# A transformer layer on eight cores: the attention product is copied off its PSUM bank before it is scaled, the prologue works in token halves, and projections, weight buffers and transposes are re-ordered

## The chip, the cores and the metric

The kernel runs on the 8 NeuronCores of one Trainium2 chip, two dies of four cores. Every core computes one of the 8 batch entries with the same program and no core talks to another. The metric is the time of the slowest core in microseconds (us), as measured on the device; several executions are timed and the median is quoted. Engines are named as the profile names them: PE is TensorE (its weight loads are PEld), DVE is VectorE, ACT is ScalarE, POOL is GpSimd, SP is SyncE. SP and POOL only issue DMAs here; an issue on such a queue is written SPq or POOLq. Each engine runs its instructions strictly in program order and waits on semaphores.

## The reference

Per core: x is 2048 tokens by 2048 features in float32. Attention has 16 heads of 128. Half of each head's features is rotated (RoPE) in the queries and keys. The feed-forward block has 5632 hidden features and integer weights that are read as (w - 128) * scale.

```python
q, k, v = (proj(wq), proj(wk), proj(wv))
q, k = apply_rope(q, k, sin, cos)
att = jnp.einsum('bhqd,bhkd->bhqk', q, k) * (1.0 / math.sqrt(HD))
att = jax.nn.softmax(att, axis=-1)
y = jnp.einsum('bhqk,bhkd->bhqd', att, v)
y = y.transpose(0, 2, 1, 3).reshape(b, t, c)
return y @ wo.T
...
gate = jax.nn.silu(_qlinear(x, wq_gate, s_gate))
up = _qlinear(x, wq_up, s_up)
return _qlinear(gate * up, wq_down, s_down)
...
x = _layernorm(x + _L0_attn_ref(...))
x = _layernorm(x + _L0_ffn_ref(...))
```

## The kernel before

The program is written by hand, engine by engine; the order in the source is the order on the engine. One array AB in SBUF holds all tiles at hand-chosen byte offsets, and PS is the PSUM, used as eight banks of 128x512 float32. So the profile calls nearly every operand AB or PS, and the line tells what it is. All matmuls are 128x128 by 128x512 in bfloat16; there are 14656 of them. The stages, in order of time:

**Prologue.** POOL loads the weights wv and wk of head 0, then the transposed input xT in 16 tiles of 128 features by 2048 tokens (L388), casting to bfloat16. PE accumulates V and K of head 0 in all eight banks as the tiles arrive (L448, 128 matmuls), then makes the queries of head 0 (64 matmuls of L455).

**Attention.** There are 64 blocks m of 512 queries (4 per head), each of 8 slots of 256 keys, so 512 slots s. In a slot PE computes the scores of the next slot (2 matmuls, L480, banks 0 to 3), then 6 matmuls of a projection job (L455, banks 6 and 7), then the product of the probabilities with V (2 matmuls, L522), which accumulates over the 8 slots of a block in bank 4 or 5 by the parity of m. A job is 16 matmuls and makes 512 tokens of Q, K or V of the next head; the last head has none. ACT takes the exponential of the scores (L620) into a ring of 8 buffers P and copies each finished job to SBUF (L645). DVE adds the exponentials up (L734, L738, L743), rotates Q and K (L696 to L706), and scales the product (L727).

The softmax denominator of block m goes a long way: PE sums over the keys with a matmul by ones (`key_sums`, L491) in slot 9 after the block's start, into the job bank that is idle then; ACT copies one row of it (`sums_row`, L627); SP spreads that row over partitions (L281); DVE takes the reciprocal (`recip`, L720, slot 12); SP stores it to HBM (L285) and loads it back broadcast to 128 partitions (L292, the tile RB); DVE multiplies bank 4 or 5 by RB (`y_scale`, L727, slot 15) and so frees the bank. The next-but-one block starts on that bank in slot 16, and its first product matmul waits for the multiplication:

```python
if k == 0:
    if m >= 2:
        t.wait_ge(dve_y, m - 1)
```

SP stores y to HBM and at the end loads it back for all heads as YTB (L304). V jobs are written transposed, and SP turns them with DMA transposes (L256).

**Output projection.** 16 token tiles of 64 matmuls (L544) with the weights WO; the last eight of those are loaded in one burst when the jobs are done (L407). DVE adds x and takes the layer-norm sums, ACT normalises, SP and POOL store the result in float32 (x1f) and bfloat16 (x1b), and SP loads it back transposed (X1T, L331).

**Feed-forward, twice for 1024 tokens each.** Gate and up projections, 44 x 64 matmuls (L565, L571), then the down projection in 4 passes of 352 matmuls (L578). The down weights arrive in 44 tiles in a ring of 4 buffers (POOL, L438), and DVE subtracts 128 from each (L768). At the start of the first half's down projection SP issues 16 DMA transposes in a row, which bring X1T for the second half (L351); behind them on SP stand the stores and loads of the residual (L356, L346) for which DVE's additions wait (L830). In the last pass DVE finishes each tile of 128 tokens alone: scale, add, statistics, wait for ACT's square root, then normalise one half while ACT normalises the other (`finish_tile`, L679, L867).

## Time and profile before

| | |
|---|---|
| time, median of 3 runs | 3418.36 us (3415.16, 3418.36, 3443.7) |
| the profiled execution | 3445.24 us, with a span of 3443.7 us on its slowest core |
| spans of the 8 cores in it | 3367.0 to 3443.7 us |
| matmuls | 14656, busy 3216.7 us, 93% of the span |
| DVE, ACT, POOL busy | 38%, 23%, 6% of the span |
| wait of PE ended by DVE's L727 | 111.4 us before L522 and 5.2 us before L544 |
| wait of PE ended by DVE's L768 | 37.4 us |

The profile describes one execution on its slowest core, core 1. Matmuls are pipelined: each shows some 380 ns of busy time, and in an unbroken stream one starts about every 216 ns. The busy share of PE over the whole span is a mean over stages that differ, so the stages are looked at one by one below.

### The profile page before, as it was taken

How to read it: one execution, taken by the hardware profiler on the slowest of the kernel's cores; microseconds unless marked ns; L12 is line 12 of the kernel's file. 1: busy time of each engine (PE TensorE's matmuls, PEld its weight loads, DVE VectorE, ACT ScalarE, POOL GpSimd, SP SyncE). 2: the span in 40 equal slices, each digit the busy share in tenths (PEclk: the TensorE clock that was granted, in tenths of full speed). 3: DMA queues.
4: the chain of work that ended last, by engine and by line, in shares of the span. 5: the costliest groups of instructions: out<-in, count | busy, mean ns of one | idle time of the engine just before them, and what ended most of it. 6: DMA issues, size and time to landing. Idle time of an engine off the chain costs nothing.

```text
span 3443.7 us, 40018 instructions; the slowest of 8 cores (3367.0 to 3443.7 us)
## 1 busy us (share of the span) xinstructions
PE 3216.7 (93%) x14656; PEld 1436.6 (42%) x14656; DVE 1311.1 (38%) x1504; ACT 804.6 (23%) x904; POOL 205.2 (6%) x364
## 2 busy tenths in 40 slices
PE   6998999999999957999999999969999999999997
PEld 2443443444444422444444444434444444444443
DVE  1665665666666643342111121022232221121334
ACT  0554554555555541111000000000010000000001
POOL 1000000000000000000100100000000001000000
PEclk9999999999999988999999999989999999999998
DMA  9333333333233154996555655996556655433555
GB/s 159 47 52 50 64 53 50 55 52 54 51 51 47 27 98 129 253 240 126 78 80 76 98 76 80 93 127 127 110 135 147 147 103 106 74 62 57 103 111 158
DMA packets 189534, 327.50 MB, mean 95 GB/s; under 512 B 97952, under 2 KB 114336, under 8 KB 183072
## 3 DMA queue, kind: packets, MB, share of 16 engines
q0 software_dynamic: 51840, 188.77, 34.4%
q1 hardware_dynamic: 137504, 136.17, 18.3%
q8 instruction: 123, 2.02, 0.3%
q14 instruction: 67, 0.55, 0.1%
HBM read 429.47 MB, written 58.85 MB: 142 GB/s over the span
## 4 chain that ended last, share of the span: by engine, by line
PE 75%; DMA 13%; SPq 4%; DVE 3%; issue 3%; ACT 1%; POOL 0%; DVEq 0%; ACTq 0%; another core or an unknown queue 0%; POOLq 0%
PE PS L565 18%; PE PS L571 18%; PE PS L578 14%; PE PS L455 11%; DMA AB<-rl_sp 8%; PE PS L544 6%; PE PS L522 4%; PE PS L480 4%; SPq L351 4%; DMA rl_sp<-AB 3%; DMA AB<-xT 1%; DMA AB<-AB 1%; ACT AB L620 1%; DVE AB L727 1%; DVE AB L738 1%
## 5 line engine op out<-in xcount | busy, mean ns | idle before, releaser
L455 PE MATMUL PS<-AB 128*128 128x512 bf16 x2944 | 722.8, 383 | 1.5 <-DVE AB L685 1.5
L620 ACT ACTIVATE AB<-PS 128x1024 bf16<-128x1024 f32 x512 | 524.2, 1025 | 574.3 <-PE PS L480 556.5
L578 PE MATMUL PS<-AB 128*128 128x512 bf16 x2816 | 615.8, 382 | 40.2 <-DVE AB L768 37.4
L565 PE MATMUL PS<-AB 128*128 128x512 bf16 x2816 | 623.8, 380 | 2.5 <-DVE AB L764 2.5
L571 PE MATMUL PS<-AB 128*128 128x512 bf16 x2816 | 622.1, 379 | 0.0
L738 DVE TENSOR_TENSOR AB<-AB 128x1024 f32<-128x1024 f32 x384 | 469.8, 1223 | 302.8 <-ACT AB L620 298.4
L795 DVE SCALAR_TENSOR_TENSOR AB<-PS,AB 128x1024 bf16<-128x1024 f32 x88 | 113.0, 1284 | 963.4 <-PE PS L571 963.4
L455 PEld LDWEIGHTS PS<-AB 128*128 128x128 bf16 x2944 | 290.0, 99 | 355.7 <-issue 13.3
L578 PEld LDWEIGHTS PS<-AB 128*128 128x128 bf16 x2816 | 276.6, 98 | 379.1 <-issue 52.3
L669 ACT ACTIVATE AB<-PS,AB 128x1024 f32<-128x1024 f32 x88 | 98.2, 1116 | 1433.8 <-PE PS L565 1433.8
L522 PE MATMUL PS<-AB 128*128 128x512 bf16 x1024 | 312.8, 388 | 120.6 <-DVE AB L727 111.4
L565 PEld LDWEIGHTS PS<-AB 128*128 128x128 bf16 x2816 | 275.9, 98 | 336.1 <-issue 5.2
L571 PEld LDWEIGHTS PS<-AB 128*128 128x128 bf16 x2816 | 275.5, 98 | 332.4
L480 PE MATMUL PS<-AB 128*128 128x512 bf16 x1024 | 310.9, 386 | 0.0
L544 PE MATMUL PS<-AB 128*128 128x512 bf16 x1024 | 225.5, 384 | 5.2 <-DVE AB L727 5.2
L768 DVE TENSOR_SCALAR AB<-AB 128x2048 bf16<-128x2048 bf16 x88 | 60.3, 692 | 391.3 <-DMA AB<-wd_c 391.3
L522 PEld LDWEIGHTS PS<-AB 128*128 128x128 bf16 x1024 | 97.1, 99 | 260.7 <-issue 159.6
L544 PEld LDWEIGHTS PS<-AB 128*128 128x128 bf16 x1024 | 101.1, 99 | 129.4 <-issue 11.4
L480 PEld LDWEIGHTS PS<-AB 128*128 128x128 bf16 x1024 | 101.7, 99 | 127.1 <-issue 11.1
L410 POOL DMA_DIRECT2D AB<-wg_c x88 | 46.6, 529 | 1089.0 <-PE PS L571 1089.0
L645 ACT CAST AB<-PS 128x512 bf16<-128x512 f32 x180 | 105.1, 584 | 11.0 <-PE PS L455 11.0
L727 DVE TENSOR_TENSOR AB<-PS,AB 128x512 bf16<-128x512 f32 x64 | 44.1, 690 | 123.2 <-DMA AB<-rl_sp 123.1
(60 smaller groups left out, 995.4 us busy)
## 6 DMA issues: line engine op xcount, KB each, us to landing
AB<-wg_c POOLq DMA_DIRECT2D x88, 512.0 KB, 5.8
AB<-wu_c POOLq DMA_DIRECT2D x88, 512.0 KB, 8.9
AB<-wd_c POOLq DMA_DIRECT2D x88, 512.0 KB, 6.0
AB<-rl_sp SPq DMA_DIRECT2D x64, 256.0 KB, 5.6
...
```

The costliest lines, as they stand in the source:

```text
L351: s_.dma_start_transpose(X1T[:, di * 1024:(di + 1) * 1024], x1b[1024:2048, di * 128:(di + 1) * 128]).then_inc(x1t_ld[di], 16)
L455: mm = t.matmul(bank(6 + G % 2)[:, 0:512], W[wi % NW][:, di * 128:(di + 1) * 128], XT[:, di * 2048 + c * 512:di * 2048 + (c + 1) * 512], s ...
L480: mm = t.matmul(bank(2 * (u % 2) + kk)[:, 0:512], KT[h % 2][:, (2 * k + kk) * 128:(2 * k + kk + 1) * 128], QT[h % 2][:, (m % 4) * 512:(m % ...
L522: mm = t.matmul(bank(4 + m % 2)[:, 0:512], V[h % 2][:, (2 * k + kk) * 128:(2 * k + kk + 1) * 128], P[s % NP][:, kk * 512:(kk + 1) * 512], ...
L544: mm = t.matmul(bank((tt % 2) * 4 + c)[:, 0:512], YTB[cq % 2][:, y * 512 + (tt % 4) * 128:y * 512 + (tt % 4 + 1) * 128], WO[y][:, c * 512: ...
L565: mm = t.matmul(bank(par * 4 + c)[:, 0:512], GW[i % 3][:, di * 128:(di + 1) * 128], X1T[:, di * 1024 + c * 512:di * 1024 + (c + 1) * 512], ...
L571: mm = t.matmul(bank(par * 4 + 2 + c)[:, 0:512], UW[i % 3][:, di * 128:(di + 1) * 128], X1T[:, di * 1024 + c * 512:di * 1024 + (c + 1) * 512],
L578: return t.matmul(bank(tt)[:, 0:512], HT[:, h2 * 1024 + tt * 128:h2 * 1024 + (tt + 1) * 128], WD[gi % 4][:, (h2 % 4) * 512:(h2 % 4 + 1) * ...
L620: sc.activation(P[u % NP], bank(2 * (u % 2), 2)[:, 0:1024], AF.Exp, bias=-C_SHIFT, scale=ASCL).then_inc(act_exp, 1)
L645: sc.copy(dst, bank(6 + G % 2)[:, 0:512]).then_inc(act_job, 1)
L738: v.tensor_tensor(ACC[m % 2], ACC[m % 2], P[s % NP], AL.add).then_inc(dve_acc, 1)
L795: v.scalar_tensor_tensor(HT[:, ht * 1024:(ht + 1) * 1024], bank((i % 2) * 4 + 2, 2)[:, 0:1024], SUC[:, ht:ht + 1], GS[i % 2], AL.mult, AL. ...
```

## The change

The attention product is no longer scaled out of PSUM. In slot 9 of a block ACT copies the bank as it is to a float32 tile YU (three of them), PE then puts the key sums into that same bank in slot 12, and ACT copies the row out in slot 13, which frees the bank. The reciprocal and the scaling come in slots 20 and 29, from SBUF. The prologue loads xT in two halves of 1024 tokens and makes K, V, Q of head 0 and K of head 1 for each half, 256 matmuls. The remaining 176 jobs are spread over 480 slots (5.77 matmuls each), with three of them, the last query chunks of head 15, left for the last head's slots. The order of the jobs within a head changes, and rotation is done in chunks of 512 tokens, each in the slot after its job. WO tiles 8 to 15 go into buffers of the attention stage as these become free, and the blocks 60 and 61 are scaled straight into YTB. Three smaller edits: the gate and up tiles 1 and 2 are loaded later in the output projection; the 16 transposes of the first down projection are issued one for every second group of weights; and the second half's down weights have a ring of 8. In the last pass ACT normalises both halves of the tile before, except for the last tile.

```diff
+    def jobs_of(h):
+        if h == 1:
+            return [(h, k, c) for k in "VQ" for c in range(4)]
+        if h < 10:
+            return [(h, k, c) for k in "VKQ" for c in range(4)]
+        return ([(h, "K", c) for c in range(4)] + [(h, "Q", 0)] + [(h, "V", c) for c in range(4)]
+                + [(h, "Q", c) for c in range(1, 4)])
...
+    def filled(s):
+        if s <= 480:
+            return s * (16 * NJ - 48) // 480
+        return 16 * NJ - 48 + min(48, 4 * min(s - 480, 4) + 2 * max(0, s - 484))
...
@@ sync, first down projection
-            for di in range(NDI):
-                s_.dma_start_transpose(X1T[:, di * 1024:(di + 1) * 1024],
-                                       x1b[1024:2048, di * 128:(di + 1) * 128]).then_inc(x1t_ld[di], 16)
+            for gi in range(5 * NG):
+                p, gq = divmod(gi, NG)
+                if gi % 2 == 0 and gi < 2 * NDI:
+                    if gq == 0:
+                        if p >= 1:
+                            s_.wait_ge(pe_dn, 8 * p)
+                    else:
+                        s_.wait_ge(pe_wd, (NG - 1) * p + gq)
+                    s_.dma_start_transpose(X1T[:, gi // 2 * 1024:(gi // 2 + 1) * 1024],
...
@@ gpsimd
+            for hf in range(2):
+                for di in range(NDI):
+                    if hf == 1:
+                        g.wait_ge(xt_ld[di], 16)
+                    g.dma_start(out=XT[:, di * 2048 + hf * 1024:di * 2048 + (hf + 1) * 1024],
...
-                if tt == 2:
-                    for i in range(3):
-                        gu_load(i)
+                if tt == 2:
+                    for i in range(3):
+                        g.wait_ge(y_st[i], y_stored(NM - 1, i))
+                    gu_load(0)
+                if tt == 11:
+                    gu_load(1)
+                    gu_load(2)
...
@@ tensor
             def key_sums(m):
+                t.wait_ge(act_yu, m + 1)
                 t.wait_ge(dve_acc, 8 * (m + 1))
-                s = 8 * m + 9
-                t.wait_ge(act_job, job_at(s) if s < 32 * (NH - 1) else 184)
-                if m >= 1:
-                    t.wait_ge(act_l, m)
-                t.matmul(bank(l_bank(m))[:, 0:512], ONB, ACCB[m % 2], start=True, stop=True).then_inc(pe_l, 1)
+                t.matmul(bank(4 + m % 2)[:, 0:512], ONB, ACCB[m % 2], start=True, stop=True).then_inc(pe_l, 1)
...
-                        t.wait_ge(dve_y, m - 1)
+                        t.wait_ge(act_l, m - 1)
...
@@ scalar
+            def y_out(m):
+                sc.wait_ge(pe_pv, 8 * (m + 1))
+                if m >= 3:
+                    sc.wait_ge(dve_y, m - 2)
+                sc.copy(YU[m % 3], bank(4 + m % 2)[:, 0:512]).then_inc(act_yu, 1)
...
+                if k == 1 and m >= 1:
+                    y_out(m - 1)
+                if k == 5 and m >= 1:
+                    sums_row(m - 1)
...
@@ vector
-                if k == 4 and s >= 12:
-                    recip((s - 12) // 8)
-                if k == 7 and s >= 15:
-                    y_scale((s - 15) // 8)
+                if k == 4 and 20 <= s < 20 + 8 * NM:
+                    recip((s - 20) // 8)
+                if k == 5 and 29 <= s < 29 + 8 * NM:
+                    y_scale((s - 29) // 8)
```

How the order changes on three engines. In each row stand the line, the operation, what it writes and reads, and the semaphores for which it waits.

PE before, from the last job matmuls of a block's last slot into the next block. dve_y counts the scalings, act_l the copied rows of key sums, act_exp the exponentials:

```order
L455 MATMUL PS<-AB 128x512 [waits act_job,act_l]
L455 MATMUL PS<-AB 128x512 x5
L522 MATMUL PS<-AB 128x512 [waits act_exp,dve_y]
L522 MATMUL PS<-AB 128x512
L480 MATMUL PS<-AB 128x512 [waits act_exp]
L480 MATMUL PS<-AB 128x512
L491 MATMUL PS<-AB 128x512 [waits dve_acc,act_job,act_l]
L455 MATMUL PS<-AB 128x512 x6
L522 MATMUL PS<-AB 128x512 [waits act_exp]
```

PE of the change in the same place, and four slots on (L600 is the product, L571 the scores, L552 a job, L579 the key sums; act_yu counts the copies of the product):

```order
L552 MATMUL PS<-AB 128x512 x6
L600 MATMUL PS<-AB 128x512 [waits act_exp,act_l]
L600 MATMUL PS<-AB 128x512
L571 MATMUL PS<-AB 128x512 [waits act_exp]
...
L552 MATMUL PS<-AB 128x512 x5
L579 MATMUL PS<-AB 128x512 [waits act_yu,dve_acc]
L600 MATMUL PS<-AB 128x512 [waits act_exp]
```

The wait for the scaling is gone from the first product matmul, and the key sums have moved back by three slots and wait for ACT's copy.

DVE before, in one block (rb_ld is the landing of RB, lq_ld that of the spread row):

```order
L720 RECIPROCAL AB<-AB 128x4 [waits lq_ld0,rl_st0]
L738 TENSOR_TENSOR AB<-AB 128x1024 [waits act_exp,dve_acc] x3
L743 TENSOR_TENSOR AB<-AB 128x512 [waits dve_acc,pe_l]
L727 TENSOR_TENSOR AB<-PS,AB 128x512 [waits pe_pv,rb_ld0,y_st0]
L734 TENSOR_TENSOR AB<-AB 128x1024 [waits act_exp]
```

DVE of the change (L804 is the reciprocal, L816 the scaling, L829 and L834 the additions):

```order
L804 RECIPROCAL AB<-AB 128x4 [waits lq_ld1]
L829 TENSOR_TENSOR AB<-AB 128x1024 [waits act_exp,dve_acc]
L816 TENSOR_TENSOR AB<-AB 128x512 [waits act_yu,rb_ld0]
L829 TENSOR_TENSOR AB<-AB 128x1024 [waits act_exp,dve_acc] x2
L834 TENSOR_TENSOR AB<-AB 128x512 [waits dve_acc,pe_l]
```

Before, reciprocal and scaling in a block belong to the same denominator, three slots apart; now the scaling in a block belongs to the denominator whose reciprocal was taken one block and one slot earlier.

SP before, at the start of the first down projection (L351 the transposes, L356 and L346 the residual's stores and loads):

```order
L351 DMA_TRANSPOSE AB<-x1b 128x1024 [waits pe_gu]
L351 DMA_TRANSPOSE AB<-x1b 128x1024 x15
L356 DMA r_sp<-AB 128x512 [waits dve_ad]
L346 DMA AB<-x1f 128x512
L356 DMA r_sp<-AB 128x512 [waits dve_ad]
L346 DMA AB<-x1f 128x512
```

SP of the change (L398 the transposes, L404 and L386 the residual's stores and loads):

```order
L398 DMA_TRANSPOSE AB<-x1b 128x1024 [waits pe_gu]
L398 DMA_TRANSPOSE AB<-x1b 128x1024 [waits pe_wd] x5
L404 DMA r_sp<-AB 128x512 [waits dve_ad]
L386 DMA AB<-x1f 128x512
...
L398 DMA_TRANSPOSE AB<-x1b 128x1024 [waits pe_wd]
L404 DMA r_sp<-AB 128x512 [waits dve_ad]
```

The first residual traffic now stands behind 6 transposes, each held back until PE has gone two weight groups further, and not behind 16 in a row.

## Rows read from the trace of the kernel before

**Rows 1.** The page: span, and busy time of PE, its share and matmuls.

```profile
span 3443.7 us, 40018 instructions; the slowest of 8 cores (3367.0 to 3443.7 us)
...
PE 3216.7 (93%) x14656; PEld 1436.6 (42%) x14656; DVE 1311.1 (38%) x1504; ACT 804.6 (23%) x904; POOL 205.2 (6%) x364
```

**Rows 2.** Spans and mean granted clock of two of the cores.

```profile
core 1: 3443.7 us, clock 0.979
...
core 6: 3367.0 us, clock 0.985
```

**Rows 3.** Core 1: stretch, length, busy (instructions) of PE, PEld, DVE, ACT, POOL, clock, DMA.

```profile
0.00:80.50 80.50, 46.52 (x193) 18.40 (x194) 12.21 (x18) 4.91 (x5) 12.48 (x27) 1.00 1.01 164
80.50:1227.70 1147.20, 1072.75 (x4869) 476.67 (x4868) 738.16 (x723) 613.93 (x722) 27.98 (x54) 0.99 0.32 50
1227.70:1321.00 93.30, 39.06 (x126) 12.48 (x125) 38.99 (x39) 31.92 (x34) 2.08 (x4) 0.74 0.64 128
1321.00:1551.50 230.50, 225.34 (x1026) 101.14 (x1026) 84.19 (x127) 36.37 (x32) 11.18 (x21) 0.98 0.87 214
1551.50:2159.30 607.80, 607.80 (x2818) 275.55 (x2817) 115.05 (x138) 52.70 (x47) 58.85 (x91) 1.00 0.56 87
2159.30:2503.50 344.20, 308.94 (x1409) 138.12 (x1407) 83.17 (x125) 0.00 (x0) 22.56 (x42) 0.96 0.82 113
2503.50:3113.00 609.50, 609.46 (x2816) 275.96 (x2817) 135.52 (x166) 51.88 (x47) 46.40 (x86) 1.00 0.52 109
3113.00:3443.70 330.70, 306.85 (x1409) 138.26 (x1407) 103.84 (x170) 12.87 (x17) 23.64 (x40) 0.96 0.53 112
```

**Rows 4.** Core 1, the first 35 us of attention, same columns.

```profile
80.00:115.00 35.00, 35.00 (x164) 15.85 (x163) 22.60 (x23) 20.57 (x24) 1.58 (x3) 1.00 0.28 48
```

**Rows 5.** Waits of PE between 80.5 and 1227.7: total, times, longest.

```profile
PE PS L522 <- DVE AB L727: 74.2, 40, 5.7
```

**Rows 6.** Waits of PE between 1227.7 and 1345.

```profile
PE PS L522 <- DVE AB L727: 37.2, 3, 17.9
PE PS L491 <- DVE AB L743: 8.0, 1, 8.0
```

**Rows 7.** DMAs of one line, issue to landing: of L292 (RB), then of L304 (YTB).

```profile
DMA to landing us min/median/max: 3.1/5.6/9.9
...
DMA to landing us min/median/max: 10.6/10.8/11.0
```

**Rows 8.** Groups: exponential, addition, scaling, one step of a 512-token rotation.

```profile
L620 ACT ACTIVATE AB<-PS 128x1024 bf16<-128x1024 f32 x512 | 524.2, 1025 | 574.3 <-PE PS L480 556.5 <-DVE AB L738 8.5 <-DVE AB L743 5.5
L738 DVE TENSOR_TENSOR AB<-AB 128x1024 f32<-128x1024 f32 x384 | 469.8, 1223 | 302.8 <-ACT AB L620 298.4 <-DVE AB L738 0.5
...
L727 DVE TENSOR_TENSOR AB<-PS,AB 128x512 bf16<-128x512 f32 x64 | 44.1, 690 | 123.2 <-DMA AB<-rl_sp 123.1
L706 DVE TENSOR_TENSOR AB<-AB 64x512 bf16<-64x512 bf16 x4 | 1.7, 418 | 0.4
```

**Rows 9.** Prologue in order of time: start, duration, idle time before in brackets.

```profile
17.27 8.13 PE L448 MATMUL PS<-AB 128*128 128x512 bf16 x24 [17.27 <-DMA AB<-xT]
...
63.27 1.89 PE L448 MATMUL PS<-AB 128*128 128x512 bf16 x8 [1.38 <-DMA AB<-xT]
```

**Rows 10.** First down projection of core 1: SP's transposes, and PE's longest stall.

```profile
2159.51 124.02 SPq L351 DMA_TRANSPOSE AB<-x1b  x16
...
2305.26 25.09 PE L578 MATMUL PS<-AB 128*128 128x512 bf16 x105 [24.44 <-DVE AB L768]
```

**Rows 11.** The same transposes on core 2.

```profile
2138.03 62.78 SPq L351 DMA_TRANSPOSE AB<-x1b  x16
```

**Rows 12.** The end on core 1: last matmuls, and DVE taking the last two tiles.

```profile
3396.81 30.41 PE L578 MATMUL PS<-AB 128*128 128x512 bf16 x128 [7.37 <-DVE AB L768]
...
3430.67 0.68 DVE L823 TENSOR_TENSOR AB<-PS,AB 128x512 f32<-128x512 f32 x1
...
3434.97 0.69 DVE L823 TENSOR_TENSOR AB<-PS,AB 128x512 f32<-128x512 f32 x1
```

518 lines of the change are left out of this document (282 added, 236 removed).

## The prediction

> **What bounds the kernel now.** I read the page's first lines, then the table by stage, then the waits inside the two stages where PE falls short, and last the single stalls of the down projection. PE is the bound: 14656 matmuls, busy 93% of 3443.7 us [rows 1]. The pace of an unbroken stream is read from the first gate and up stage, 2818 matmuls in 607.8 us at granted clock 1.00, so 0.2157 us each [rows 3]. At that pace all matmuls take 3161 us; some 280 us of the span are something else, and the table by stage says where they lie [rows 3]. The second gate and up stage, 609.5 us, has nothing in it. The 480 slots of heads 0 to 14 (80.5 to 1227.7) hold 4869 matmuls, 1050 us of pace, and take 1147: 97 us over. The last head and the way to the output projection (1227.7 to 1321.0) take 93.3 us for 126 matmuls, 27 us of pace. The first down projection takes 344.2 for 304 us of pace, and the last stretch, second down projection and end, 330.7 for 304. The prologue takes 80.5.
>
> In attention one thing is waited for: the scaling L727, 74.2 us in 40 waits before the last head, and 37.2 us in 3 waits in it, the longest 17.9 [rows 5, 6]. The scaling itself waits for the load of RB: DVE stood 123.1 us for it [rows 8], and that load takes 3.1 to 9.9 us where the source leaves it one slot of some 2.2 us [rows 7]. Without such a wait the pace is reached: the first 35 us of attention have PE busy throughout [rows 4]. The 22 us that remain of the 97 are matmuls at half clock, since the stretch shows 1072.75 us busy for 1050 us of work [rows 3].
>
> The cores differ by these waits: spans 3443.7 and 3367.0 at clocks 0.979 and 0.985 [rows 2]. So I build the new time up by stages instead of subtracting a share.
>
> **The change, part by part.** *Prologue.* Tile by tile xT lands every 3.07 us ((63.27 - 17.27) / 15, [rows 9]). Two weights and one tile land by 17.27, so the stream starts at 8.1. With four weights and half a tile PE starts at 8.1 + 4.5 x 3.07 = 21.9. Then 256 matmuls take 55.2, the slow first 24 cost 8.13 - 5.2 = 2.9 more [rows 9], and handing the banks over between the halves, where ACT and DVE first copy 1024 columns of each product out (1.0 to 1.2 us apiece, [rows 8]), some 1.5. That gives 81.5 against 80.5. The last half tile lands at 8.1 + 20 x 3.07 = 69.5, before PE needs it, so PE and no longer DMA is the limit, and 64 matmuls have moved in here for 1 us.
>
> A rule weighed: the trace shows no xT load under 1 MB. The Trainium skill (DMA: Bandwidth & Descriptors, Bandwidth) says to batch DMAs to 1 MiB or more, and its table has 78% efficiency at 1 MB and 32% at 64 KB; a half tile of 512 KB would lie between, and an estimate of 65% from that page makes the stream a fifth slower, its last half tile due at about 80 us and the prologue 2 us longer. By the rows it costs nothing.
>
> *480 slots.* 1920 score and product matmuls, 2768 of jobs and 59 key sums are 4747, so 1024 us. The waits for L727 go: the bank is now freed by ACT in slot 13 of 16. What comes instead are ACT's copy in slot 9 and PE's wait for it in slot 12, three slots or 6 us later; behind that wait on PE stand the next product and scores. On DVE the scaling stands 9 slots, 19 us, after its reciprocal, against RB's 9.9 at worst plus its store [rows 7]. DVE has room: 420 additions x 1.223, 120 short ones x 0.69, and 120 rotations x 4 x 0.418 make 797 us of 1024 [rows 8], 78%. ACT: 480 x 1.025, and some 290 short copies, which the trace shows only beside the rest (613.93 us busy in this stretch before, [rows 3]); with 60 product copies at 0.6 it comes to about 650, 63%. I add 6 us for leftovers (the 19 us of slack against 9.9): 1030, a gain of 117. Bounds: 1024 if nothing waits; 1085 if half of the 97 us stays.
>
> *Last head to output projection.* PE has 180 matmuls and key sums, 40 us; ACT 32 x 1.025 and 15 copies, 41; DVE 28 x 1.223, 8 x 0.69 and 3 rotations x 1.67, 45 [rows 8]. PE may run some slots ahead of DVE (8 buffers). The output projection also needs YTB, issued near slot 20 of 32, at about 29 us, landing in 10.8 [rows 7]: 40. Bounds: 43 if the engines overlap ideally, 70 if the loads of WO, YTB and x on one stretch delay the small DMAs as much as now. I take 50, near the engines' sums, since the three long waits [rows 6] all were for the scaling or what stood behind it. A gain of 43.
>
> *Output projection.* 1024 matmuls are 221; before 230.5 [rows 3]. The burst of gate and up loads shrinks early, but tiles 1 and 2 now load among the transposes, where DMA is full. I allow 3 us for a slow start and 3 for late transposes: 227, gain 3.5. Bounds 221 and 238 (the transposes late by the 4 MB that moved, 4 x 3.07 us, [rows 9]).
>
> *First down projection.* SP spent 124.02 us on the 16 transposes [rows 10], 62.78 on another core [rows 11]. Behind them stood the loads for DVE's additions, so DVE came late to the next weights: 24.44 us in one stall [rows 10]. Spread, a transpose costs 124 / 16 = 7.8 us at most and has 13.8 us (64 matmuls). The stage becomes 304 + 4 for small stalls: 308, gain 36. Bounds 304 and 344. DVE's additions in pass 2 need loads that SP issues between transposes; if a transpose is late, they are too.
>
> *End.* The ring of 8 removes the wait of 7.37 before the last 128 matmuls [rows 12]. DVE took the last tile at 3434.97, 7.8 us after PE's end at 3427.2, since a tile costs it 4.3 us (3434.97 - 3430.67) against PE's 16 x 0.2157 = 3.45; half a tile's normalisation is 1024 columns, 1.0 us at least by the rows of that size [rows 8], so 3.3 are left and DVE keeps up. ACT does both halves of tile 6 before the last half, 2 to 3 us more. So 16.5 us after PE's end become about 12, and the stage 304 + 12 = 316 against 330.7: gain 14. Bounds 312 and 324.
>
> *Sum.* 81.5 + 1030 + 50 + 227 + 607.8 + 308 + 609.5 + 316 = 3230. The profiled execution has 1.5 us outside its span (3445.24): 3231. Every term but the waits is the same on all cores, and of eight the slowest counts: 4 us more, **3235**. That is 210 under the profiled execution and 183 (5.4%) under the median of 3418.36, which is 27 us shorter than the profiled one; I don't subtract these 27 again, since they are waits that go.
>
> **Rivals.** *Half of the waits stay in attention*, because RB, its store and SP's own waits queue behind V's transposes: for it speaks RB's spread of 3.1 to 9.9 [rows 7], against it 19 us of slack. 1085 instead of 1030: 3290.
>
> *The end of attention stays a chain*: YTB ahead of the small DMAs in SP's queue, 70 instead of 50: 3255.
>
> *Spreading does not help*, as the weights starve for bandwidth and not for SP's order: +30, 3265. Against it: core 2 with short transposes.
>
> *The waits change their name*: ACT's copy or key sums hold PE as the scaling did, and the 480 slots keep their 97 us over pace: 3235 + 91 = 3326.
>
> *DVE becomes the bound, and the kernel is slower than before.* Place: the blocks of heads 1 to 14. A block has 8 x 2.13 = 17.1 us; DVE needs 797 / 60 = 13.3. If its waits inside a block (two rotations each waiting for ACT's copy of a job that ended just before, and RB) exceed 3.8 us, PE waits. It must reach 6.8 us a block for 60 x 3.05 = 183 us, 3418. With 7.5 us: 3235 + 60 x 3.7 = 3457. Against it: before, DVE had the same additions and waited 2 us a block for RB.
>
> *The clock.* A denser stream could be granted less. The lowest mean of a stretch with PE busy nine tenths is 0.96 [rows 3]: 1030 / 0.96 adds 43, 3278. It would be slower than before under 0.85. The Trainium skill (TensorE: Matmul & The Clock Gate, Part 1) says that a die goes to 13/16 of the clock once three of its cores run dense matmuls; by that the 480 slots alone would take 237 us more, 3472. The rows speak against it: 607.8 us without a gap at 1.00 [rows 3].
>
> **How the numbers follow.** Forecast 0.73; half of the waits 0.08; chain at the end 0.05; spreading useless 0.05; waits renamed 0.03; DVE bound 0.03; clock 0.03. The forecast's own bounds are 3216 (all lower bounds but the prologue's) to 3262. The range takes in the chain at the end, the useless spreading and the clock at 0.96, up to 3280; half of the waits (0.08), renamed waits and DVE stay out, 0.14 in all. A measurement here tells about 1% (34 us) from no change. Faster by over 1%, below 3384: all but DVE bound and the clock's worse half, 0.95; slower by over 1%: 0.04; within: 0.01.
>
> **What would show it.** Right: the attention product waits for nothing of the scaling, the 480 slots take 1024 to 1040 at clock 1.00; DVE near 78% busy there; output projection starts about 1162; the first down projection at 306 to 310 with no stall over 3 us; no stall in the last pass. Wrong: a new releaser before the product or the key sums; DVE's wait for RB; a stall before the first gate matmul. What would make me wrong most is the order on SP: it holds V's transposes, RB and YTB, and any of its waits holds all behind it.

## The result, and the profile after

The changed kernel takes 3295.64 us in the median of four executions (3285.52 to 3324.71), the kernel before, run beside it, 3431.03 (3415.16 to 3466.31). The ratio is 0.961 with a 95% interval of 0.950 to 0.971: faster. The forecast was 3235 and its range ended at 3280, so the sign was right and the size wrong: 135 us were won against the median beside it, and 123 against the 3418.36 from which the forecast counted its 183. Executions in which half of the chip was disturbed occur with most kernels here, e11's profiled one among them; they are left out of the ratios and counts below, which leaves 5 of 11 executions of the kernel before beside e13, e14 and e16.

The page and the spans of all cores; the profiled execution is the one of 3285.52 us:

```profile
span 3284.0 us, 40569 instructions; the slowest of 8 cores (3236.6 to 3284.0 us)
...
PE 3166.0 (96%) x14363; PEld 1434.7 (44%) x14656; DVE 1347.7 (41%) x1871; ACT 835.9 (25%) x970; POOL 209.2 (6%) x380
```

```profile
core 0: 3236.6 us, clock 0.996
core 1: 3260.7 us, clock 0.993
core 2: 3284.0 us, clock 0.990
core 3: 3242.1 us, clock 0.996
core 4: 3256.2 us, clock 0.993
core 5: 3244.3 us, clock 0.994
core 6: 3250.7 us, clock 0.994
core 7: 3245.6 us, clock 0.996
```

Core 0 stands 7 us above the forecast's sum of 3230, core 2 54 us above it. The table by stage of core 2, the slowest, with the columns of [rows 3] (some 2% of PE's records are missing here, so counts and busy times of PE are a little low):

```profile
0.00:81.60 81.60, 57.82 (x252) 25.03 (x258) 10.52 (x20) 4.54 (x5) 21.18 (x44) 1.00 0.94 146
81.60:1118.00 1036.40, 1023.99 (x4662) 465.77 (x4758) 777.57 (x1080) 634.57 (x774) 28.53 (x55) 1.00 0.37 58
1118.00:1166.80 48.80, 39.91 (x168) 16.05 (x170) 39.69 (x48) 34.91 (x42) 1.29 (x3) 0.97 0.67 133
1166.80:1391.30 224.50, 220.36 (x1006) 100.22 (x1027) 89.04 (x134) 36.88 (x33) 10.67 (x20) 1.00 0.90 226
1391.30:2014.20 622.90, 608.04 (x2761) 275.64 (x2816) 116.04 (x138) 52.59 (x47) 54.53 (x92) 0.99 0.48 89
2014.20:2360.70 346.50, 308.55 (x1382) 138.76 (x1409) 82.80 (x125) 0.00 (x0) 23.72 (x42) 0.96 0.83 113
2360.70:2968.40 607.70, 604.75 (x2760) 275.50 (x2817) 135.51 (x166) 51.76 (x47) 47.88 (x90) 1.00 0.56 113
2968.40:3284.00 315.60, 302.58 (x1380) 137.69 (x1407) 96.52 (x163) 20.64 (x24) 21.40 (x36) 0.99 0.50 110
```

Against the terms of the sum, in order: 81.6 (81.5 forecast), 1036.4 (1030), 48.8 (50), 224.5 (227), 622.9 (607.8), 346.5 (308), 607.7 (609.5), 315.6 (316). Five terms hold within 2.5 us. The excess of 54 us is 6.4 + 15.1 + 38.5 less small change, and each part has a wait. PE's waits on core 2, first in the 480 slots, then in the last head, in gate and up, and in the first down projection (total, times, longest, as in [rows 5]):

```profile
PE PS L600 <- DMA AB<-AB: 7.4, 1, 7.4
PE PS L571 <- DVE AB L791: 0.5, 1, 0.5
...
PE PS L600 <- DMA AB<-AB: 4.2, 1, 4.2
PE PS L600 <- ACT AB L700: 3.0, 6, 0.8
PE PS L571 <- DVE AB L786: 1.5, 1, 1.5
...
PE PS L645 <- DMA AB<-x1b: 11.9, 3, 7.2
...
PE PS L658 <- DVE AB L910: 26.3, 2, 22.2
PE PS L658 <- DVE AB L855: 7.6, 2, 6.8
```

The 40 waits for the scaling [rows 5] are gone, and none of their kind has taken their place: the scaling (now L816) itself waits 0.2 us in all where it waited 123 [rows 8]. The first row is something else, the product L600 waiting once, from 92 us on, for V's transposes. L645 (gate) waits for the transposes of the first token half. L658 (down) waits for DVE, and the next rows, DVE in the middle of that stage, show for what:

```profile
2156.75 0.69 DVE L855 TENSOR_SCALAR AB<-AB 128x2048 bf16<-128x2048 bf16 x1 [7.93 <-DMA AB<-wd_c]
2170.19 0.69 DVE L855 TENSOR_SCALAR AB<-AB 128x2048 bf16<-128x2048 bf16 x1 [12.75 <-DMA AB<-wd_c]
2188.10 0.69 DVE L855 TENSOR_SCALAR AB<-AB 128x2048 bf16<-128x2048 bf16 x1 [17.21 <-DMA AB<-wd_c]
2188.70 4.87 DVE L910 TENSOR_TENSOR AB<-PS,AB 128x512 f32<-128x512 f32 x8
```

PE's longest stall (22.2 us, until 2189.5) is put down to L910, the bank's emptying, but L910 ran at once when its turn came. Ahead of it in DVE's program stood the dequantisation L855, and that waited 17.2 us for a load of down weights. So the releaser that is named was done for when something else arrived.

What the loads waited for is a question of the transfers. Landing times in the first down projection, of the transposes (L398) and of the down weights (L484), on core 0 and then on core 2:

```profile
DMA to landing us min/median/max: 3.0/6.9/13.3
DMA to landing us min/median/max: 4.9/6.0/10.8
...
DMA to landing us min/median/max: 6.2/22.4/39.7
DMA to landing us min/median/max: 5.1/9.9/34.0
```

And the transfer queues in the same 66 us (2124 to 2190) of both cores, core 2 first:

```profile
DMA packets 6931, 7.46 MB, mean 113 GB/s; under 512 B 4912, under 2 KB 4912, under 8 KB 6928
q1 hardware_dynamic: 5761, 3.16, 75.5%
q0 software_dynamic: 1167, 4.26, 47.9%
...
DMA packets 8119, 10.13 MB, mean 153 GB/s; under 512 B 4908, under 2 KB 4908, under 8 KB 8116
q0 software_dynamic: 1330, 4.79, 46.7%
q1 hardware_dynamic: 6786, 5.29, 28.6%
```

Both have five transposes in that stretch, some 4900 small packets. The hardware queue q1 carries them and the loads and stores of the residual; on core 2 it takes 75.5% of the transfer engines' time for 3.16 MB, on core 0 28.6% for 5.29 MB, over four times as much per byte. Sorted by size, the same two traces show which packets it is. The 256-byte packets of the transposes took 149 ns in the mean on core 2 (4530 of them, 63.9% of the engines' time) and 23 ns on core 0 (4368, 9.7%), with a median of 18 ns on both: a part of them took very long. The 2048-byte packets of the residual took 97 and 96 ns. Over the whole stage the mean of the 256-byte packets goes with the stage's length: 24 to 39 ns on the three cores that took 306.5 us, 48 to 59 on the four with 315 to 327, 93 on core 2 with 346. The weights share the engines with them.

For the experiments the stages are compared over all eight cores, by the start times of the stages' first matmuls in the trace. Means of the eight in us (boundaries as above), the slowest core of the first down projection, and the mean span:

| kernel | 480 slots | last head | output + first gate/up | first down, mean / slowest | last stage | mean span |
|---|---|---|---|---|---|---|
| before | 1126.8 | 87.0 | 833.9 | 325.8 / 344.3 | 332.8 | 3396.9 |
| changed | 1036.9 | 49.9 | 840.7 | 317.6 / 346.4 | 317.2 | 3252.5 |
| e0 | 1037.1 | 50.9 | 850.4 | 319.5 / 337.1 | 321.4 | 3270.8 |
| e1 | 1036.9 | 51.7 | 855.6 | 307.2 / 310.7 | 320.5 | 3263.0 |
| e2 | 1037.3 | 49.7 | 840.7 | 329.4 / 340.4 | 319.0 | 3267.0 |
| e3 | 1037.3 | 51.1 | 847.5 | 325.1 / 355.9 | 316.8 | 3269.1 |
| e4 | 1037.6 | 50.3 | 846.9 | 324.5 / 331.0 | 317.2 | 3267.2 |
| e5 | 1049.7 | 79.6 | 830.7 | 337.1 / 356.4 | 330.1 | 3317.6 |
| e6 | 1026.4 | 52.2 | 854.5 | 325.0 / 338.4 | 321.1 | 3269.9 |
| e8 | 1037.3 | 49.8 | 843.0 | 313.4 / 325.2 | 319.1 | 3253.7 |
| e10 | 1026.4 | 51.0 | 838.7 | 311.6 / 328.5 | 319.9 | 3239.1 |
| e12 | 1037.0 | 50.5 | 846.2 | 316.5 / 327.4 | 318.8 | 3260.1 |
| e13 | 1026.4 | 51.2 | 835.7 | 312.2 / 323.3 | 319.2 | 3236.1 |
| e14 | 1037.3 | 49.9 | 839.0 | 322.5 / 341.5 | 317.7 | 3257.3 |
| e16 | 1026.4 | 52.6 | 854.9 | 313.4 / 324.3 | 319.5 | 3257.5 |

e11 has no row, since its profile has only cores 0 to 3 to compare. Each stage figure comes from one profiled execution.

The times, and "low pair": in how many of the executions both cores of a pair (0 and 1, 2 and 3, ...) had a mean granted clock of 0.988 or less. e10, e11 and e12 ran on one chip, e13, e14 and e16 on another.

| kernel | executions, us | ratio to before | low pair |
|---|---|---|---|
| changed | 3285.5, 3324.7, 3301.7, 3289.6 | 0.961 (0.950 to 0.971) | 3 of 4 |
| e0 | 3309.6, 3289.4 | | 2 of 2 |
| e1 | 3279.8, 3267.8, 3282.9 | 0.961 (0.954 to 0.967) | 3 of 3 |
| e2 | 3277.4, 3293.5 | 0.963 (0.954 to 0.972) | 1 of 2 |
| e3 | 3306.5, 3288.1, 3306.7 | 0.968 (0.961 to 0.975) | 3 of 3 |
| e4 | 3304.4, 3278.6, 3327.3, 3293.4 | 0.962 (0.950 to 0.974) | 3 of 4 |
| e5 | 3342.1, 3327.7, 3329.3, 3331.0 | 0.971 (0.963 to 0.979) | see e5 |
| e6 | 3289.8, 3299.7, 3305.6 | 0.962 (0.947 to 0.977) | 3 of 3 |
| e8 | 3270.8, 3310.0, 3312.2 | 0.961 (0.946 to 0.976) | 2 of 3 |
| e12 | 3286.5, 3296.9, 3282.8 | 0.963 (0.959 to 0.968) | 2 of 3 |
| e10 | 3257.6, 3289.8, 3254.1, 3266.7, 3245.7 | 0.956 (0.951 to 0.961) | 1 of 5 |
| e11 | 3254.6, 3254.5, 3280.4, 3253.1 | 0.956 (0.950 to 0.961) | 0 of 4 |
| e14 | 3274.0, 3272.4, 3270.4, 3283.4, 3273.7 | 0.957 (0.954 to 0.960) | 0 of 5 |
| e16 | 3272.3, 3266.7, 3282.7, 3282.6, 3272.0, 3281.8 | 0.958 (0.954 to 0.961) | 6 of 6 |
| e13 | 3247.4, 3253.6, 3247.4, 3249.2 | 0.950 (0.946 to 0.953) | 0 of 4 |

### The profile page after: what moved, and what is told of

It reads as the page before. It is cut to its first block, busy times and chain, and to the rows that moved or that the text cites. A ratio compares the mean times of both kernels' runs of the same rounds, so it can differ in the third digit from the quotient of the medians.

```text
span 3284.0 us, 40569 instructions; the slowest of 8 cores (3236.6 to 3284.0 us)
## 1 busy us (share of the span) xinstructions
PE 3166.0 (96%) x14363; PEld 1434.7 (44%) x14656; DVE 1347.7 (41%) x1871; ACT 835.9 (25%) x970; POOL 209.2 (6%) x380
## 4 chain that ended last, share of the span: by engine, by line
PE 90%; DMA 6%; SPq 2%; issue 1%; DVE 1%; ACT 0%; POOL 0%; ACTq 0%; DVEq 0%; POOLq 0%
PE PS L651 18%; PE PS L645 18%; PE PS L552 18%; PE PS L658 17%; PE PS L600 6%; PE PS L571 6%; PE PS L624 4%; DMA AB<-wd_c 2%; SPq L370 2%; PE PS L537 1%; DMA AB<-AB 1%; DMA AB<-xT 1%; DMA AB<-x1f 1%; DMA rl_sp<-AB 0%; PE PS L579 0%
## 5 line engine op out<-in xcount | busy, mean ns | idle before, releaser
L552 PE MATMUL PS<-AB 128*128 128x512 bf16 x2760 | 685.0, 380 | 3.0
L658 PE MATMUL PS<-AB 128*128 128x512 bf16 x2759 | 611.0, 381 | 37.0 <-DVE AB L910 26.3
L645 PE MATMUL PS<-AB 128*128 128x512 bf16 x2760 | 620.9, 380 | 17.4 <-DMA AB<-x1b 11.9
L651 PE MATMUL PS<-AB 128*128 128x512 bf16 x2760 | 619.6, 379 | 2.9
L829 DVE TENSOR_TENSOR AB<-AB 128x1024 f32<-128x1024 f32 x384 | 468.6, 1220 | 168.1 <-ACT AB L700 162.1
L658 PEld LDWEIGHTS PS<-AB 128*128 128x128 bf16 x2816 | 276.6, 98 | 371.1 <-issue 42.9
L645 PEld LDWEIGHTS PS<-AB 128*128 128x128 bf16 x2816 | 275.2, 98 | 349.0 <-issue 17.9
L552 PEld LDWEIGHTS PS<-AB 128*128 128x128 bf16 x2816 | 275.9, 98 | 333.5 <-issue 2.4
L651 PEld LDWEIGHTS PS<-AB 128*128 128x128 bf16 x2816 | 276.0, 98 | 333.3 <-issue 1.9
L600 PE MATMUL PS<-AB 128*128 128x512 bf16 x1007 | 302.1, 380 | 15.7 <-DMA AB<-AB 11.6
L571 PE MATMUL PS<-AB 128*128 128x512 bf16 x1001 | 300.4, 380 | 3.1 <-DVE AB L786 1.5
L624 PE MATMUL PS<-AB 128*128 128x512 bf16 x1004 | 220.4, 379 | 4.1 <-DVE AB L863 1.9
L855 DVE TENSOR_SCALAR AB<-AB 128x2048 bf16<-128x2048 bf16 x88 | 59.1, 692 | 321.0 <-DMA AB<-wd_c 320.9
L600 PEld LDWEIGHTS PS<-AB 128*128 128x128 bf16 x1024 | 99.4, 98 | 138.9 <-issue 22.9
L571 PEld LDWEIGHTS PS<-AB 128*128 128x128 bf16 x1024 | 100.3, 98 | 124.4 <-issue 4.7
L624 PEld LDWEIGHTS PS<-AB 128*128 128x128 bf16 x1024 | 100.1, 98 | 122.8 <-issue 2.6
L825 DVE TENSOR_TENSOR AB<-AB 128x1024 f32<-128x1024 bf16 x64 | 78.2, 1222 | 66.1 <-ACT AB L700 65.8
```

Of the source, the lines that this page charges most:

```text
L552: mm = t.matmul(bank(6 + n % 2)[:, 0:512], W[wi % NW][:, di * 128:(di + 1) * 128], XT[:, di * 2048 + c * 512:di * 2048 + (c + 1) * 512], s ...
L571: mm = t.matmul(bank(2 * (u % 2) + kk)[:, 0:512], KT[h % 2][:, (2 * k + kk) * 128:(2 * k + kk + 1) * 128], QT[h % 2][:, (m % 4) * 512:(m % ...
L600: mm = t.matmul(bank(4 + m % 2)[:, 0:512], V[h % 2][:, (2 * k + kk) * 128:(2 * k + kk + 1) * 128], P[s % NP][:, kk * 512:(kk + 1) * 512], ...
L624: mm = t.matmul(bank((tt % 2) * 4 + c)[:, 0:512], YTB[cq % 2][:, y * 512 + (tt % 4) * 128:y * 512 + (tt % 4 + 1) * 128], WO[y][:, c * 512: ...
L645: mm = t.matmul(bank(par * 4 + c)[:, 0:512], GW[i % 3][:, di * 128:(di + 1) * 128], X1T[:, di * 1024 + c * 512:di * 1024 + (c + 1) * 512], ...
L651: mm = t.matmul(bank(par * 4 + 2 + c)[:, 0:512], UW[i % 3][:, di * 128:(di + 1) * 128], X1T[:, di * 1024 + c * 512:di * 1024 + (c + 1) * 512],
```

## Experiments

**e0_again: the changed kernel once more.**

> The changed kernel once more, to see which of its stage times repeat. Three theories of why its first down projection takes 304 us on some cores and up to 344 on others. Order: the transposes and the loads and stores of the residual on one issuing engine (SyncE) hold each other up, and the next weights with them. Slow transposes: a transpose reads pieces of 256 bytes from rows 4 KB apart, some take 20 to 40 us where most take 6, and meanwhile they starve the weight loads on the shared DMA engines. Chance: it was one disturbed execution. By the first two, again several cores over 304 us, not necessarily the same ones, and a slowest core of 3270 to 3300 us. By the third, all cores 304 to 308 and 3240 to 3250.

Measured: it repeats, on other cores. First down projection 307 to 337 us, the slowest core 1 this time. It was not chance. But what made cores 0 and 1 the last was new: both spent 248 to 257 us in the output projection, against 222 to 230 on the others. Core 0 in two stretches of that time (columns as before, the third number from the end is the granted clock):

```profile
1187.00:1309.00 122.00, 121.20 (x458) 50.55 (x465) 39.64 (x60) 17.36 (x15) 4.80 (x9) 0.81 0.73 197
1309.00:1340.00 31.00, 30.84 (x143) 14.02 (x144) 10.71 (x16) 4.59 (x4) 1.06 (x2) 1.00 0.65 193
```

PE has no gap in either, but 458 matmuls take 121 us, 0.265 each, and then 143 take 31, 0.216 each. The grant was 0.81, between the two levels of 1.2 and 2.4 GHz, and neither the trace of the kernel before nor the changed kernel's first one has such a stretch. So two disturbances had to be told apart from here on: the transfers and the clock.

**e1_no_transposes.**

```
-  s_.dma_start_transpose(X1T[:, ...], x1b[1024:2048, ...]).then_inc(x1t_ld[gi // 2], 16)
-  t.wait_ge(x1t_ld[di], 16 * (th + 1))
+  t.wait_ge(x1t_ld[di], 16)
```

> The 16 transposes of the second half are left out, so the second 1024 tokens are computed from the first half's input. Order and Slow transposes both say: first down projection 304 to 308 us on every core, slowest core 3245 to 3260 us. If the weights starve on their own (loads of 0.5 MB for gate, up and down against each other), some core stays at 320 or more.

Measured: first down projection 306.5 to 310.7 on all eight, mean 307.2. So weights and residual alone starve nobody, and the stage's excess belongs to the transposes. The slowest core was outside what was expected (3278 instead of 3245 to 3260), since cores 0 to 3 all had 0.81 in the output projection.

**e2_pitch.**

```
-  x1b = nc.dram_tensor("x1b", [T, D], ...)
+  x1b = nc.dram_tensor("x1b", [T, D + 128], ...)
```

> The rows that the transposes read stand 4352 bytes apart instead of 4096. Slow transposes (the pitch makes their pieces meet in one place of memory): every transpose lands in 6 to 8 us, the first down projection takes 304 to 308 us on all cores, the wait before the first gate matmul falls under 3 us, slowest core about 3240. Order: no difference, some cores again 315 to 345 us.

Measured: mean 329.4, slowest 340.4, seven of eight cores over 312. The transposes landed in 12.9 to 21.0 us in the median of a core, where the changed kernel has 6.2 to 8.7 on seven cores and 22.4 on core 2. Output projection with gate and up stays at the changed kernel's 840.7, so the wait before the first gate matmuls did not go either. This pitch makes nothing better; whether it makes things worse one profile does not tell. That the pitch of 4096 bytes is the culprit has nothing left that speaks for it.

**e3_burst.**

```
+  for di in range(NDI):
+      s_.dma_start_transpose(X1T[...], x1b[1024:2048, ...]).then_inc(x1t_ld[di], 16)
   for gi in range(5 * NG):
-      if gi % 2 == 0 and gi < 2 * NDI: ... (one transpose)
```

> Only the spreading is undone: all 16 transposes are issued at once before the residual's traffic, as in the kernel before. Order: the first down projection takes 320 to 340 us on seven of eight cores as before, the slowest core 3275 to 3300 us, and the mean of the eight is 10 us or more above the changed kernel's. Slow transposes: the same slowest core (about 340 us for the stage), and the mean of the eight only some 8 us above.

Measured: mean 325.1, slowest 355.9. The burst kernels (before, e3, e5) have means of 325.8, 325.1 and 337.1, the spread ones (changed, e0, e6, e12, e14) 317.6, 319.5, 325.0, 316.5 and 322.5. By these eight profiles spreading is worth some 9 us of the mean, 329.3 against 320.2, and little on the slowest core: 344 to 356 against 327 to 346. The size is uncertain: e3, the only one that differs from the changed kernel in this alone, lies at e6's value, and 5.6 to 7.5 us above the two profiles known when its expectation was written. That is less than the 10 of the first theory and near the 8 of the second.

**e4_on_act: the transposes from ACT's queue.**

```
+  sc.wait_ge(pe_wd, (NG - 1) * p + gq)        (ACT, at the same places)
+  sc.dma_start_transpose(X1T[...], x1b[1024:2048, ...]).then_inc(x1t_ld[di], 16)
```

> The 16 spread transposes are issued by ACT, which has nothing else to do in the first down projection; the residual's loads and stores stay on SyncE. Same times of issue, same bytes. Order (the transposes hold the residual's traffic up in SyncE's queue, that holds DVE up, and DVE the weights): mean of the eight cores' first down projections 306 to 309 us against 317.6 and 319.5 of the two executions of the changed kernel, slowest core of the stage under 312. Shared engines (the transposes slow every other transfer whoever issues them): mean 315 to 325, some core over 330.

Measured: mean 324.5, slowest 331.0; transposes still up to 36.3 us. Both figures are those expected of shared engines. SyncE's order, my theory in the prediction, is not what holds the stage: with nothing behind the transposes in their queue, the stage is as before.

**e8_wider.**

```
+  TR_AT = [round(2.75 * j) for j in range(NDI)]
-      if gi % 2 == 0 and gi < 2 * NDI:
+      if gi in TR_AT:
```

> The 16 transposes are spread over 41 of the 44 weight groups of the first down projection (one in 19 us) instead of 30 (one in 13.8 us). If they and the weights merely share the transfer rate: mean of the stage 308 to 312 us over the eight cores, slowest under 325. If a transpose is slow by a state that a core falls into, whatever the spacing: mean 317 or more, slowest over 335.

Measured: mean 313.4, slowest 325.2: just over the edge of what sharing was to give, clearly under what a state of the core was. It repeats: e10, e13 and e16, which have the same spacing, show 311.6, 312.2 and 313.4, every one under all five of the narrower spacing. Single transposes still take up to 44.6 us, so spacing lessens the collision and does not remove the cause.

**e5_before_yu: the kernel before with the unscaled copy alone.**

```
+  def y_out(m):                                       (ACT, slot 8m + 9)
+      sc.copy(YU[m % 3], bank(4 + m % 2)[:, 0:512]).then_inc(act_yu, 1)
-  v.tensor_tensor(YST[m % 3], bank(4 + m % 2)[:, 0:512], RB[m % 2], AL.mult)
+  v.tensor_tensor(YST[m % 3], YU[m % 3], RB[m % 2], AL.mult)      (slot 8m + 29)
```

> The kernel before with one part of the change: the product is copied off its bank unscaled by ACT and scaled later from that copy, with the key sums, their reciprocal and the scaling moved to later slots as in the changed kernel. If this part is what the gain comes from: 480 slots of heads 0 to 14 near 1030 us (mean 1127 before, 1037 changed; less work is left in them since the queries stay in the last two heads, so 1020 to 1050 either way), the stretch of the last head no shorter than 75 us, whole kernel 3300 to 3330 us. If the attention was held by the other parts (jobs placed otherwise, ring of buffers): 480 slots over 1080 us, whole kernel 3360 or more. The output projection, which used to start after a chain of waits, shows whether a granted clock of 0.81 there comes with the unbroken attention ahead of it: yes by that theory on some cores, in none if it needs the shortened last head.

Measured: mean span 3317.6, so 79 of the 144 us by which the means differ come from this part: 77 in the 480 slots, 7 in the last head and 6 in other stages, less 11 by a longer first down projection, whose code is that of the kernel before. The 480 slots take 1049.7, which is the 1050 that the prediction gave as the bare pace of their matmuls. Core 0's list of PE's waits is empty for them; the last head has these:

```profile
PE PS L540 <- DMA AB<-y_sp: 16.0, 1, 16.0
PE PS L519 <- DMA AB<-AB: 13.8, 1, 13.8
PE PS L490 <- DVE AB L751: 6.2, 2, 5.8
```

The rest of the change lies in the last head (79.6 to 49.9), the last stage (330.1 to 317.2), the spreading, and the queries moved. It also shows a loss: output projection and first gate and up take 830.7 here and 840.7 in the changed kernel, which loads the weights of tiles 1 and 2 behind token tile 11 where they used to be loaded behind tile 2; that this place is the reason was not tested by putting it back. No core's profile has 0.81 here. (Its mean clocks say nothing: all lie at 0.982 to 0.989, from stretches at half clock behind its waits.)

**e6_calm: two bursts of loads moved.**

```
-  if tt == 11: gu_load(1); gu_load(2)
+  if tt == 14: gu_load(1)
+  if tt == 15: gu_load(2)
...
+  if wi == 6:                      (POOL, weights of attention)
+      g.wait_ge(vt_ld[2], 16); g.wait_ge(vt_ld[3], 16)
```

> Two loads are moved: the gate and up weights of tiles 1 and 2 behind token tiles 14 and 15 instead of both behind tile 11, and the third and later weights of attention behind the first head's V transposes. Collision theory (a burst of weight loads stretches the transposes issued beside it from some 6 to 18 us, and PE waits for them): the wait before the first gate matmuls falls from 3 to 12 us to under 2, output projection plus first gate and up from a mean of 840.7 to 832 to 835 us; PE's wait near 92 us falls from 6.5 to 9.5 to under 3, and the 480 slots from 1037 to 1028. Rival: the transposes are slow by themselves, and neither wait moves by more than 2 us; or the wait only changes its name, to the gate weights of tile 1 (output projection plus gate and up still 840).

Measured: one half as expected and one half not. The 480 slots fall from 1037 to 1026.4, the same on all eight cores (1028 expected). In the other place the wait changed its name, as the rival said; core 0:

```profile
PE PS L649 <- DVE AB L854: 7.2, 1, 7.2
PE PS L649 <- DMA AB<-x1b: 2.3, 1, 2.3
```

L854 is the dequantisation of tile 1's gate weights, now late. On cores 0 to 5, which had the full clock, output projection and gate and up took 847.9 us in the mean, 6 more than on the same cores of the changed kernel. The V transposes, the other half, did become prompt: the first two of the first head landed in 5.6 to 7.8 us on the eight cores, against 15.7 to 20.3.

**e12_again, e10_four, e11_pause: four edits together, and the clock.** e10 has e6's edit for V, e8's spacing, and these two; e11 has the last line in place of the WO edit:

```
   elif y < 14:                     (POOL, WO loads 12 and 13)
+      for c in range(4): g.wait_ge(vt_ld[c], 16 * NH)
       g.wait_ge(pe_s, 32 * (NH - 1))
...
   if tt == 11: gu_load(1)
+  if tt == 15: gu_load(2)
...
+  for c in range(4) if s == 32 * (NH - 1) else (k // 2,):      (e11: PE, first product of the last head)
       t.wait_ge(vt_ld[c], 16 * (h + 1))
```

> The changed kernel a third time, to be compared on one chip with the next two, and to count the granted clock of 0.81. In the profiles so far, pairs of neighbouring cores (0 and 1, 2 and 3, 4 and 5, 6 and 7) had 0.81 for some 160 us from the middle of the last head, in e0_again one pair, e1 two, e3 one, e4 one, e6 one, in the first profile, e2 and e8 none, and in e5 (long pauses at the end of attention) none. A pair that has it ends 25 to 30 us later at a mean clock of .98. Expected: at least half of the executions have such a pair, median 3285 to 3305 us, attention 1037, first down projection 316 to 325 in the mean.

> Four edits of the changed kernel at once, each in a stage of its own: (1) weights of attention from the third on wait for the first V transposes, as in e6; (2) the WO loads 12 and 13 wait for the last head's V transposes, so that the last of these takes 2.4 us as the others do, not 14; (3) the gate and up weights of tile 1 stay behind token tile 11, those of tile 2 go behind tile 15; (4) the transposes of the second half spread as in e8. Collision theory: 480 slots 1026.4; last head to output projection 44 to 46 against 49.9; output projection with gate and up 834 to 838 (840.7 changed, 848 in e6); first down projection 308 to 316 in the mean; mean of the eight spans 3225 to 3235, and where no core is at 0.81 a slowest core of 3235 to 3250. Rival on the clock: a stream without any stall at the end of attention is granted 0.81 more often, in every execution, and the slowest core stays at 3265 to 3285. Rival on names: tile 1 or 2 arrives late and DVE's gate dequantisation holds PE as in e6.

> As e10, but without its second edit, and with a pause instead: the first product of the last head waits for all four V transposes (the last lands 14 us after its issue), so PE stands some 11 to 13 us once at about 1110 us, as long as the pause that the kernel of e5 has there. If such a pause keeps the grant at full clock: no pair at 0.81 in any execution, last head to output projection 55 to 60 us, slowest core 3245 to 3260, and a median below e10's. If it does nothing for the clock: pairs at 0.81 as often as in e10 and e12, slowest core 3275 to 3295, median above e10's by 10 us.

Measured: e12 is as expected, with a low pair in two of three. e10 was faster than e12 on the same chip in four of five executions, 3246 to 3267 against 3283 to 3297; the fifth, with a low pair, took 3290. Attention and down projection came as expected. The mean span of its profile, 3239, and the slowest core, 3256, lie above what was expected. The last head did not shorten: the last V transpose lands in 6.0 to 8.6 us where the changed kernel has 14.1 to 15.9, but the product then waits up to 5.3 us for ACT. Output projection with gate and up, 838.7, is just over what was expected. On the clock the rival fell: with no wait for V, 0.81 became rarer, not more frequent. e11 has it in none of four, with a median of 3254.6 against e10's 3257.6, although attention and last head take 9 us more than in e10 (cores 0 to 3 of its profile). The pause stands in the 480 slots by the boundaries used here; core 0:

```profile
PE PS L607 <- DMA AB<-AB: 12.9, 1, 12.9
```

**e14_second_only, e16_without_second, e13_five: what the clock hangs on, and the first half's transposes.** e14 is the changed kernel with the WO lines alone, e16 is e10 without them. e13 is e10 with

```
-  if 9 <= tt <= 14: for di in range(3 * (tt - 9), ...)
+  if 9 <= tt <= 11: for di in range(6 * (tt - 9), ...)
```

> The changed kernel with e10's second edit alone: the WO loads 12 and 13 wait for the last head's V transposes. The wait of 4 to 6 us near 1127 us goes. Before every stretch at 0.81 so far stands such a wait, then 3 to 7 us at half clock, then 0.81 some 10 us after the wait. If the clock hangs on that: no pair, or at most one execution with one, at 0.81 (mean clock .98, span 25 to 30 us over its neighbours), ratio to before some 0.003 to 0.006 lower than the changed kernel's 0.963 of e12, slowest core 3255 to 3285. If it hangs on something else: a pair in most executions as in e12, median 3285 to 3300.

> e10 without its second edit: the wait of 4 to 6 us in the last head is back. By the first theory a pair at 0.81 in at least half of the executions and a slowest core of 3265 to 3290; by the other, as e10 (one of five), slowest 3250 to 3265.

> e10 and a fifth edit: the 16 transposes of the first half are issued behind token tiles 9 to 11 (6, 6, 4) instead of 9 to 14 (3 each), so that most stand ahead of the gate and up weights of tile 1. If their place is what makes them late: no wait before the first gate matmul, output projection plus first gate and up 830 to 833 us against 838.7 in e10; mean of the spans 3230 to 3235. If they now hold SyncE's loads of x and stores, the output projection itself grows to 226 or more and nothing is won; if the loads of tile 2 are late instead, DVE's gate dequantisation holds PE and the sum stays near 838.

Measured: no low pair in five executions of e14, one or more in each of six of e16, on one chip. Both sets of times lie in what the first theory expected. Core 1 of e16, in order of time: the last matmuls of the head's start, the wait, and the change of pace (the second number is the duration of two matmuls):

```profile
1115.38 0.59 PE L558 MATMUL PS<-AB 128*128 128x512 bf16 x2
1121.95 1.01 PE L606 MATMUL PS<-AB 128*128 128x512 bf16 x2 [5.98 <-DMA AB<-AB]
...
1126.69 0.59 PE L606 MATMUL PS<-AB 128*128 128x512 bf16 x2
...
1132.20 0.70 PE L606 MATMUL PS<-AB 128*128 128x512 bf16 x2
```

Two matmuls take 0.59 us at full clock, 1.01 at half clock behind the wait, 0.59 again, and 0.70 from 1132 on. The same core from there, and then core 6 of the same execution, which kept its clock:

```profile
1132.00:1294.00 162.00, 159.12 (x601) 64.20 (x600) 68.32 (x96) 40.26 (x43) 4.80 (x9) 0.81 0.67 184
1294.00:1325.00 31.00, 31.00 (x146) 13.99 (x143) 12.24 (x17) 4.59 (x4) 1.06 (x2) 1.00 0.68 218
...
1132.00:1294.00 162.00, 153.86 (x706) 67.81 (x705) 80.18 (x112) 43.84 (x47) 5.34 (x10) 1.00 0.81 204
```

In 162 us the one did 601 matmuls, the other 706. The 105 fewer are 23 us of pace, most of the 25 to 30 us by which a low pair ends later. All such stretches in the profiles (e0 one pair, e1 two, e3, e4, e6 and e12 one, e16 three) are 162 to 163 us long and begin 7 to 10 us after the end of this wait, which was 4.8 to 7.8 us on those cores. Over all kernels that keep this wait, 28 of 33 executions have a low pair. Over e10, e13 and e14, which do not have it, one of 14.

How far this goes: the edit that takes the wait away decides, nearly always, whether a low pair comes. e14 and e16 differ in more than that edit; the comparisons that differ in it alone, e14 with the changed kernel (7 of 9 over its three runs) and e10 with e16, are each between two chips. That the wait is the cause is not shown. It is not enough by itself: cores 6 and 7 of e16 had it too, 5.2 us each, and kept 1.00, and so did cores 0 to 5 of e6 with 4.9 to 7.6 us. Nor does every wait of that length bring it: in e10 and e13 PE waited up to 5.3 us for ACT some 20 us later, without 0.81. The edit also moves two weight loads in time; e11, which leaves those loads where they were and has the longer pause, speaks against the loads as the cause.

e13 is the best: 3247.4 to 3253.6, ratio 0.950 against the changed kernel's 0.963 in e12 on another chip, and below every execution of e14 and e16 on its own. Its mean span is 3236.1, just over the 3230 to 3235 expected. PE on core 0 waits for nothing in gate and up, but the mean of output projection with gate and up is 835.7, not 830 to 833. All three cases of the expectation came true, on different cores: 831 to 832 on cores 0, 4, 6 and 7; on cores 1 and 5 the output projection grew to 233, with waits for the residual's addition of up to 5.3 us; on cores 2 and 3 the gate dequantisation held PE for 6.7 and 3.7 us.

## Why the prediction missed

*Prologue.* 81.6 us against 81.5, partly by luck. The last half tile of xT landed at 77.5 us on core 0 and 76.9 on core 2, not at 69.5: over the whole stream one landed every 1.8 us, where half of 3.07 is 1.5. That is nearer to the 80 us of the slower stream, which the prediction weighed and set aside, than to its own rows. PE needed the last half tile at about 79 us, so the lateness just fitted, and on core 2 PE waited 1.4 us for xT after its start. In the program the second half's loads also wait for the first half's, so how much of it is their size is not separated.

*Attention's waits.* Right, and the mechanism is shown: scaling and RB off the path (e5), no new releaser. One bound of the prediction was added wrongly: half of the 97 us over 1030 makes 1078 and a time of 3283, not 1085 and 3290; as no wait of that kind stayed, nothing hangs on it. I had 6 us for leftovers and expected none in particular; what came is one wait for V's transposes at 92 us with its half clock, 10.6 us by e6. Without it 480 slots are 1026.4, where the sum had 1024. The landing of V's transposes beside a burst of five weight loads was never costed; in the trace of before PE did not wait for them: there they were issued from 67.6 us on and the first product came at 83, in the changed kernel they were issued from 81 on and the first product came at 83 too.

*Last head, second gate and up, end.* 50, 609.5 and 316 against 48.8, 607.7 and 315.6 on core 2. Right by their own steps.

*Output projection and the way into gate.* "I allow 3 us for a slow start and 3 for late transposes: 227" placed the lateness in the wrong stage. The output projection took 224.5; the transposes were awaited by the first gate matmuls, 11.9 us and a half-clock stretch on core 2, 9.3 us in the mean stage. The upper bound of 238 (by its own terms nearer 236) would have had room for it; the term of 607.8 for gate and up, carried over as if it could not change, had none.

*First down projection, the step that failed.* "Spread, a transpose costs 124 / 16 = 7.8 us at most and has 13.8 us" took SyncE's time in a burst for a transpose's price. SyncE's time is that of issuing; landing is another matter, 6.9 us in the median on core 0 and 22.4 on core 2, where the weights' loads took up to 34.0 and PE stood 22.2 us in one stall. The rival "spreading does not help, as the weights starve for bandwidth and not for SP's order" had 0.05 and is what the slowest core shows: 346.5, even above its 338. In the mean of the cores, spreading gained some 9 us of the 22 that separate the burst (329.3) from the stage without transposes (307.2). My argument against the rival was core 2 of the old profile with 62.78 us [rows 11]. That was one core of eight; the two cores that I read took 344.3 (core 1) and 306.5 us (core 2) for the stage, a spread that a forecast for the slowest core had to carry over. e1 shows that the transposes are the cause, e4 that their queue is not, e2 that a pitch of 4096 bytes is not, e8 that their density is a part. Why a part of the 256-byte packets is slow, and on some cores of an execution more than on others, stays open. Whether more buffers for the down weights (four in this stage, eight in the second half) would hide it was not tried.

*"Of eight the slowest counts: 4 us more".* The mean of the eight spans is 3252.5, 22 above the sum; the slowest is 31.5 above that mean. In the profiled execution, where no core had 0.81, the first down projection makes most of it (346.4 on core 2, 317.6 in the mean); in the others the clock adds to it. The 4 us were taken from nothing. The forecast's own lower bounds add up to 3208, not 3216, which changes nothing here.

*The clock.* The rival had 0.03 and was argued away with 607.8 us at 1.00 [rows 3]. Full clock in one stage of one kernel did not tell of another stage: a grant of 0.81 came in most executions of the changed kernel, with 25 to 30 us for the pair that has it. The three executions of the changed kernel with a low pair are those of 3289.6 to 3324.7. An estimate of what the clock takes of the median is the ratio of e12, 0.963, less that of e14, 0.957, some 20 of the 61 us by which the forecast was short; the other 40 lie mostly in the waits for transfers above, and the execution of 3285.5, with no low pair, was outside the range without it. The Trainium skill (TensorE: Matmul & The Clock Gate, Part 1) gives 13/16 of the clock for a whole die, once three of its cores run dense matmuls, held while the load lasts. The level agrees with the rows here; the extent does not: a pair of cores, for 162 us, and the long dense stages at 1.00 (the second gate and up took 607.8 to 609.5 us on every core of every profile but e11's). The 3472 that I worked out by that rule would have been much too long for any execution compared here.
